# Softmax shift from TensorE to DVE, paired output products and an output bias on POOL, in a fused attention and expert layer

## What is computed

```python
x = x + tanh(g_xattn[0]) * xattn(layernorm(x), ctx)     # 16 heads of 64, causal softmax, scores / sqrt(64)
x = x + tanh(g_ffn[0])   * ffn(layernorm(x))
# ffn, per row, D = 128, 16 "heads" of 8:
h  = rmsnorm(x) * gamma1
q  = h @ Wq + bq;  k, v = split((h @ Wdown + bdown) @ Wup + bup)
att = softmax(q k / sqrt(8)) over the 16 heads of the same row
x2 = x + (att v) @ Wo + bo
h2 = rmsnorm(x2) * gamma2
out = x2 + sum_e softmax(h2 @ Wg + bg)[e] * (h2 @ We[e])   # 8 experts
```

## Time and profile before

| | us |
|---|---|
| median of 3 runs | 261.29 (259.64 to 261.53) |
| the profiled execution | 261.93 |
| its span | 259.9 |

### The profile page before, as it was taken

One profiled execution on the slowest core, in us unless ns is written; L12 is line 12 of the kernel. 1 busy time (PEld: TensorE's weight loads), 2 busy tenths in 40 slices (PEclk: granted clock), 3 DMA queues, 4 the chain that ended last, 5 costly groups with the idle time before them and its releaser, 6 DMA issues.

```text
span 259.9 us, 7887 instructions
## 1 busy us (share of the span) xinstructions
PE 245.6 (94%) x3244; PEld 178.7 (69%) x3244; DVE 192.4 (74%) x333; ACT 171.6 (66%) x501; POOL 149.9 (58%) x157
## 2 busy tenths in 40 slices
PE   7989989998899999999999999988999897979995
PEld 4765877785867677676859595858676462858774
DVE  0237644189998989898998842799989999786964
ACT  2437634756687787978787778566877676472454
POOL 4104041264646686969696835778466995867320
PEclk9999999999999999999999999999999998899999
DMA  6990000000000000000000000000000000000000
GB/s 208 359 320 21 3 4 3 3 1 3 3 3 0 3 10 3 15 0 15 1 3 13 3 11 3 13 3 10 3 0 5 11 14 3 11 0 3 10 13 20
DMA packets 6017, 7.30 MB, mean 28 GB/s; under 512 B 477, under 2 KB 4830, under 8 KB 5982
## 3 DMA queue, kind: packets, MB, share of 16 engines
q1 hardware_dynamic: 5550, 6.16, 7.5%
q10 hardware_dynamic: 432, 0.64, 0.7%
HBM read 5.88 MB, written 0.92 MB: 26 GB/s over the span
## 4 chain that ended last, share of the span: by engine, by line
PE 70%; DVE 18%; ACT 5%; issue 4%; POOL 1%; DVEq 0%; POOLq 0%
PE ps_a L875 40%; PE ps_c L875 9%; PE ps_b L875 8%; PE ps_e L875 7%; PE ps_b L927 4%; DVE ps_e L665 3%; DVE prod L683 3%; DVE ps_e L694 2%; ACT probs L446 2%; DVE nmax L626 2%; PE ps_b L872 1%; DVE psums L631 1%; DVE fqkv L649 1%; POOL prod L326 1%; PE ps_c L971 1%
## 5 line engine op out<-in xcount | busy, mean ns | idle before, releaser
L326 POOL TENSOR_TENSOR prod<-fqkv 128x1280 f32<-128x1280 f32 (+1 forms) x14 | 38.7, 2761 | 10.3 <-DVE fqkv L649 10.3
L316 POOL TENSOR_TENSOR probs<-probs,prinv 120x672 f32<-120x672 f32 x16 | 24.3, 1518 | 31.1 <-DVE prinv L635 31.1
L334 POOL TENSOR_TENSOR prod<-e_sb,fqkv 128x768 f32<-128x768 f32 (+1 forms) x14 | 24.5, 1753 | 21.3 <-ACT e_sb L474 21.3
L875 PEld LDWEIGHTS ps_a<-aT,wo_sb 128*128 128x128 f32 x256 | 30.8, 196 | 4.4 <-ACT v_sb L435 2.6
L875 PE MATMUL ps_a<-aT,wo_sb 128*128 128x112 f32 x256 | 32.1, 279 | 0.4 <-ACT aT L440 0.3
L875 PE MATMUL ps_a<-wv_sb,cT 128*64 128x512 f32 x128 | 32.3, 620 | 0.0
L665 DVE TENSOR_REDUCE ps_e<-prod 128x256 f32<-128x2048 f32 x13 | 29.7, 2287 | 0.0
L694 DVE TENSOR_REDUCE ps_e<-prod 128x128 f32<-128x2048 f32 x13 | 29.7, 2285 | 0.0
L875 PE MATMUL ps_a<-cT,wk_sb 128*128 128x224 f32 x128 | 28.6, 375 | 0.0
L429 ACT COPY kT<-ps_a 128x448 f32<-128x448 f32 x32 | 17.1, 533 | 16.2 <-PE ps_a L875 16.2
L875 PE MATMUL ps_a<-xT,wqc 128*128 128x224 f32 x128 | 27.1, 361 | 0.6 <-ACT qT L429 0.6
(11 more groups left out here) (144 smaller groups left out, 487.9 us busy)
## 6 DMA issues: line engine op xcount, KB each, us to landing
xp_sb<-in_xp SPq DMA_DIRECT2D x1, 896.0 KB, 7.9
out<-out_sb SPq DMA_DIRECT2D x14, 64.0 KB, 1.5
xT<-in_x_t SPq DMA_DIRECT2D x1, 784.0 KB, 9.5
cT<-in_ctx_t SPq DMA_DIRECT2D x1, 784.0 KB, 11.1
wv_sb<-in_wv SPq DMA_DIRECT2D x1, 512.0 KB, 8.1
wo_sb<-in_wo SPq DMA_DIRECT2D x1, 512.0 KB, 12.7
fwe_sb<-in_fwe SPq DMA_DIRECT2D x1, 512.0 KB, 8.8
fw_sb<-in_fw SPq DMA_DIRECT2D x1, 266.0 KB, 13.1
```

Of the source, the lines that this page charges most:

```text
L316: nc.gpsimd.tensor_tensor(pr[0:TG, NC:C, :, 0:S], pr[0:TG, NC:C, :, 0:S], prinv[p % 2][0:TG, NC:C, :].unsqueeze(3).to_broadcast([TG, C - N ...
L326: nc.gpsimd.tensor_tensor(o, k, q, ALU.mult).then_inc(s["prod1_pool"], 1)
L334: nc.gpsimd.tensor_tensor(o, e, v, ALU.mult).then_inc(s["prod2_pool"], 1)
L875: return nc.tensor.matmul(o, lhsT, rhs, start=start, stop=stop, skip_group_check=True)
```

## The change

Five things change, and the order of some calls around them.
1. The shift products go from TensorE. DVE adds the negated maximum, now f32, to the scores in PSUM, in place, right behind the maximum (shifted_scores).
2. The output products (new_y) go by units: pairs (0,1), (2,3), (4,5), (6,7) together, at steps 2, 4, 6 and 8, pairs 8 to 15 alone. aT is one tile of two pairs' width. new_x1 follows the units.
3. A tile starts only when its unit is there: tile 0 at step 2, tiles 1 to 13 at steps 4 to 16, so that step 3 starts none.
4. The bias product goes. ACT multiplies xc by rstd2 (scaled_x), POOL adds the bias to it (biased), and DVE's new_x2 is a plain addition.
5. Orders. POOL makes the output adds before norm, and first_scale last, behind weighted, biased and gating. In steps 14 and 15 scaled_qkv comes before weighted on DVE; in the written-out end some calls swap places.

```diff
@@ units and tiles
-def first_step(f):
-    return (128 * (f + 1) + T - 1) // T
-TILE_AT = {first_step(f): f for f in range(NT)}
-LAST_STEP = first_step(NT - 1) + 2
+DOUBLE = 8
+Y_UNITS = [(p, p + 1) for p in range(0, DOUBLE, 2)] + [(p,) for p in range(DOUBLE, NP)]
+Y_AT = {unit[-1] + 1: n for n, unit in enumerate(Y_UNITS)}
+def units_for(f):
+    return next(n + 1 for n, unit in enumerate(Y_UNITS) if (unit[-1] + 1) * T >= (f + 1) * 128)
+def tile_steps():
+    steps, last = {}, 0
+    for f in range(NT):
+        last = max(last + 1, Y_UNITS[units_for(f) - 1][-1] + 1)
+        steps[last] = f
+    return steps
@@ POOL
+            def biased(f):
+                pool.wait_ge(s["u_ready"], f + 1)
+                if f == 0:
+                    pool.wait_ge(s["wo_scaled"], 2)
+                nc.gpsimd.tensor_tensor(xc[f % XB][:, :], xc[f % XB][:, :], fw_sb[:, COL_BO:COL_BO + D], ALU.add).then_inc(s["ub_ready"], 1)
@@ POOL, steps 2 to 13
                 if fb is not None:
                     products(fb)
+                if fd is not None:
+                    outputs(fd)
                 if t < NP:
                     norm(t)
                 if fc is not None:
                     second_scale(fc)
                 if fb is not None:
                     weighted(fb)
+                    biased(fb)
+                if fc is not None:
+                    gating(fc)
                 if fa is not None:
                     first_scale(fa)
-                if fc is not None:
-                    gating(fc)
-                if fd is not None:
-                    outputs(fd)
@@ ACT
+            def scaled_x(f):
+                act.wait_ge(s["centred"], f + 1)
+                act.wait_ge(s["rstd2_ready"], f + 1)
+                nc.scalar.activation(xc[f % XB][:, :], xc[f % XB][:, :], ACT.Copy, scale=rstd2[f % XB][:, 0:1]).then_inc(s["u_ready"], 1)
@@ ACT, steps 2 to 13
                     head_exps(fb)
+                    scaled_x(fb)
                 if t < NP:
                     turned_probs(t)
+                if fc is not None:
+                    gate_exps(fc)
                 if fa is not None:
                     x1_copy(fa)
-                if fc is not None:
-                    gate_exps(fc)
                 if t < NP:
                     attended(t, 0)
+                if fc is not None:
+                    experts(fc, 0)
+                    experts(fc, 1)
+                if t < NP:
                     attended(t, 1)
@@ DVE
+            def shifted_scores(p):
+                sc = score_banks(p)[0:TG, :, 0:C * S].rearrange("p r (c k) -> p r c k", c=C)
+                dve.wait_ge(s["nmax_ready"], p + 1)
+                nc.vector.tensor_tensor(sc, sc, nmax[p % 2][0:TG, :, :].unsqueeze(3).to_broadcast([TG, 2, C, S]),
+                                        ALU.add).then_inc(s["shifted"], 1)
@@ DVE, new_x2
-                nc.vector.scalar_tensor_tensor(out=x2[f % 2][:, 0:D], in0=xc[f % XB][:, :], scalar=rstd2[f % XB][:, 0:1], in1=ps_c[:, 1, 0:D],
-                                               op0=ALU.mult, op1=ALU.add).then_inc(s["x2_ready"], 1)
+                dve.wait_ge(s["ub_ready"], f + 1)
+                nc.vector.tensor_tensor(x2[f % 2][:, 0:D], ps_c[:, 1, 0:D], xc[f % XB][:, :], ALU.add).then_inc(s["x2_ready"], 1)
@@ DVE, steps 14 and 15
                 score_max(t)
+                shifted_scores(t)
                 products(fb)
+                prob_sums(t)
                 new_x2(fc)
-                prob_sums(t)
+                new_x1(Y_AT[t])
                 norm(t)
                 logits(fb)
-                new_x1(t - 1)
                 gate_logits(fc)
                 shifted_logits(fb)
+                scaled_qkv(fa)
                 weighted(fb)
...
@@ DVE, the end
                 scaled_qkv(last)
+            shifted_logits(prior)
             products(last)
-            shifted_logits(prior)
@@ TensorE
-            def shift(p):
...
+            def new_y(n):
+                if n == 0:
+                    pe.wait_ge(s["wo_in"], 16)
                 for b in range(2):
+                    pe.wait_ge(a_free[b], USES["y", n][b])
+                if n:
+                    pe.wait_ge(s["x1T_ready"], n)
+                c0, w = Y_UNITS[n][0] % 2 * T, len(Y_UNITS[n]) * T
                 for ch in range(C):
+                    ins = mm(ps_a[:, 0, 0:w], wo_sb[:, ch, :], aT[:, ch, c0:c0 + w], start=(ch == 0), stop=(ch == C - 1))
                 ins.then_inc(s["y_made"], 1)
...
@@ TensorE, steps 2 to 13
                     scores(t)
                     values(t, 0)
-                    values(t, 1)
                 if fc is not None:
                     turn_o(fc)
                 if t < NP:
-                    shift(t)
-                if fc is not None:
-                    bias_o(fc)
+                    values(t, 1)
+                if fc is not None:
                     new_o(fc)
-                if t <= NP:
-                    new_y(t - 1)
+                if t in Y_AT:
+                    new_y(Y_AT[t])
@@ TensorE, the end
             logit_sums(prior)
+            output_sums(PE_OUT[0])
             turn_x2(third)
-            output_sums(PE_OUT[0])
+            expert_half(third, 1)
             gate_logits(third)
-            expert_half(third, 1)
```

More of the change, by code:

```diff
@@ L408, in _ @@
             gating(third)
+            biased(prior)
             weighted(last)
             second_scale(prior)
+            biased(last)
             gating(prior)
@@ L439, in attended @@
                 act.wait_ge(a_full[b], n)
[L440 removed]
+                nc.scalar.copy(aT[:, 4 * half:4 * half + 4, p % 2 * T:(p % 2 + 1) * T],
                                ps_a[:, b, 0:4 * T].rearrange("p (c t) -> p c t", c=4)).then_inc(a_free[b], 1)
@@ L541, in _ @@
                 if t < NP:
+                    values(t, 0)
                     exps(t)
@@ L587, in _ @@
             kv_copy(last)
-            x2_copy(third)
             squares(third)
             head_exps(prior)
-            late_out(PE_OUT[0])
+            scaled_x(prior)
+            x2_copy(third)
+            scaled_x(last)
             gate_exps(third)
             head_exps(last)
+            late_out(PE_OUT[0])
             experts(third, 1)
@@ L603, in _ @@
             x2_copy(last)
+            experts(prior, 1)
             experts(prior, 0)
-            experts(prior, 1)
             gate_exps(last)
@@ L850, in _ @@
             shifted_logits(last)
+            gate_sum(third)
             head_scales(prior)
-            gate_sum(third)
             normed_heads(prior)
             weighted(last)
+            head_scales(last)
             new_x2(prior)
-            head_scales(last)
             head_sums(last)
@@ L859, in _ @@
             gate_logits(prior)
+            new_x2(last)
             gate_sum(prior)
-            new_x2(last)
             gate_logits(last)
@@ L1159, in _ @@
             turn_o(prior)
-            bias_o(prior)
             new_o(prior)
```

118 lines of the change are left out of this document (49 added, 69 removed).

## The result

The changed kernel takes 264.08 us (median of 4 runs, 263.70 to 264.89); the kernel before, timed beside it, 260.47 (259.52 to 261.53). The ratio is 1.016, 95% interval 1.012 to 1.020. The prediction was 259.2 with a range up to 263.3, so the kernel is slower, by less than 2%, where I forecast about the same or faster, and it lies outside the range. The profiled execution of after was timed at 263.70; its span is 261.9 against 259.9 before. One later run of before (263.40) and one of the kernel with the first pair alone (265.38) were in a slower state of the chip and are left out of all figures.

What follows compares the result with a forecast made beforehand. Full steps were taken as TensorE-bound before, thin steps and the end as DVE-bound; afterwards DVE's work sets full steps. Step terms sum to -3.6 us, 261.29 to 257.7, plus 1.5 for one clock fall: 259.2 us, range 256.2 to 263.3.

Steps and rivals of the forecast that it cites:

- Pairs 9 to 13, five steps of 13.7: Full single-unit steps late in the kernel: 13.7 us each on 13.6 of DVE work, +0.2 us in all against 68.3.
- Wrong if full steps exceed 14.2: Stated sign of failure: a full step, from one pair's maximum to the next, longer than 14.2 us.
- loop through POOL: Query scaling, POOL's products, output adds and norm, then TensorE to the next scores: 27.4 us over two steps, 13.7 each.
- My upper bound, 14.9: Single-unit full step if the shift comes wholly on top: 13.95 + 1.04 - 0.06 us.
- TensorE's saving of 0.61 a step: Full step with a single unit: shift 0.38 and bias product 0.23 us leave TensorE, 13.95 to 13.34.
- Pair 2, +0.6: Pair 2's step, 12.0 us before: double unit for a single one and no shift, +0.6 us.
- The fall of the clock, +1.5: Thin steps 3 and 5: TensorE's clock falls to half at 1 to 2 us per fall; one counted, +1.5.
- The shift's price: DVE's new instruction on 896 elements in PSUM: 1.1 us, expected to show at 1.08 to 1.17.
- DVE over 97% busy: Expected sign: in full steps of 13.6 to 13.8 us DVE is over 97% busy and TensorE idles again.
- Before pair 2, -2.4: Prologue: unit 0 leaves, 2.02 us, with attend(1)'s 0.6 wait; two DVE shifts add 0.15; less 2.4 us.
- The end, -1.4: Pair 15 -0.6 us and the rest -0.8, from query scaling ahead of the head sums and fewer bias products.
- Rival 3: Full steps of 14.6 us, late POOL output adds and DVE not absorbing the shift: 264.9 us; chance 0.13.

Runs made afterwards that it cites:

- the first pair alone: The kernel before, with the output projections of pairs 0 and 1 as one unit in step 2; 262.30 us, ratio 1.009.
- x1 ahead: The changed kernel, with DVE making x1 ahead of the norm in steps 2 to 13, as before; 262.75 us, ratio 1.009.
- eleven heads: The changed kernel with x1 made ahead of the norm, POOL multiplying 11 instead of 10 heads in tiles 0 to 9; 265.41 us, ratio 1.019.
- the shift alone: The kernel before, with only the shift moved to DVE behind the maximum (f32 maximum); 266.10 us, ratio 1.021.
- the bias alone: The kernel before, with only the output bias changed: no bias product, ACT scales, POOL adds the bias, DVE adds the product; 264.03 us, ratio 1.013.
- eight narrow products: The changed kernel, with eight unused narrow products added ahead of pair 2's step, 32 TensorE records more; 263.54 us, ratio 1.012.
- the narrow warm-up: The changed kernel, with 28 products of 32 columns for the two wide ones of TensorE's warm-up; 275.09 us, ratio 1.055.
- both kernels of the first pair: The kernel before with pairs 0 and 1 as one unit, without (262.30 us) and with eight unused narrow products where the prologue's output products stood (259.26 us).

## Why the prediction was wrong, step by step

- **Pairs 9 to 13, five steps of 13.7: the step that failed.** They take 14.10 to 14.24 without gaps, and 14.37 on average in after. "Wrong if full steps exceed 14.2" was my own sign, and it came. Three things in it were wrong. (1) I had DVE's 13.6 of work as the length of the step. The work is 13.5 to 13.7, but DVE's own row takes 13.84 (x1 ahead): hand-overs of 0.02 to 0.1 us between instructions that need each other come on top. (2) I looked at a loop through POOL and not at the one through x1: x1 stands behind the norm, the shift and the norm are ahead of it, and the projections wait for the bank that it reads. That is 0.37 us a step (shown by the run with x1 ahead). (3) The norm beside POOL's output adds costs DVE 0.15 in after, up to 0.5 (shown by the run with eleven heads). The loop through x1 is thus 5.50 us on DVE and 8.61 on TensorE, 14.11, with the norm alone, and 14.24 with the norm at 0.53. The loop through POOL that I priced at 13.7 is not on the chain of pair 10's or 11's step; it is on that of pair 7's, which has no unit and takes 13.69 where I had 12.9 to 13.3. My upper bound, 14.9, held this, but I took the value near the lower bound, on the strength of idle time that the shift would fill. It did fill it (the run with the shift alone).
- **TensorE's saving of 0.61 a step.** The chain gives 13.64 for its row of work with x1 ahead, against 13.95: 0.31. The shift's 0.38 is real. The bias was priced 0.23 as half of 0.46 for two products; with the bias gone the output product alone takes 0.42. In before's order that is the wait for ACT's copy of oT, in whose shadow the bias product stood (the run with the bias alone). In after's order oT is there 0.6 us before the product starts (166.07 and 166.70 with x1 ahead), and why it takes 0.42 all the same is not shown. And the value products, split by turn_o, take 0.15 more. Only DVE being the bound kept this error out of the time.
- **Pair 2, +0.6.** Without its gap (the run of after with eight narrow products) the step takes 13.00 where I had 12.6, and 12.69 with the narrow warm-up; the gap is the other 1.3 to 1.7. I had no term for it, and the trace of before gave little sign of one: its only trace of it is 0.3 us in the scores ahead of pair 6. Other kernels lose more by such gaps: the first pair alone 4.45 us in three.
- **The fall of the clock, +1.5.** None in the profiled execution of after, whose pair 3 was at 1.00 with TensorE busy 9.24 of 13.17. It came in that step, at 0.88 to 0.90, in the seven other kernels here that have step 3 without a tile, and cost 1.0 to 1.2 there (in five of them the step took 14.1 to 14.2 instead of 13.17, in two the loss fell on pair 4's). The three other runs of after, at 263.9 to 264.9, had a mean clock of 0.993 where the profiled one had 1.00. So the forecast place is right for most runs, and the size, 1.5, was somewhat high. That the profiled run had none is luck. By the rule of the Trainium skill that I cited (TensorE: Matmul & The Clock Gate, "What's actually happening") step 5 would have fallen too; in no run here did it, with TensorE busy 10.0 to 10.6 of 13.6 to 13.8.
- **The shift's price.** Right: 1.10 us, within 1.08 to 1.17, no wait before new_x2, as forecast. "DVE over 97% busy" was 95% (68.2 of 71.9).
- **Before pair 2, -2.4.** -3.4; the kernels with the first pair alone have -2.0 to -3.8, with the same work. The first maximum lies at 15.4 to 16.7 us in kernels that have the same work ahead of it (15.70 in after, 16.64 in before), so up to 1.3 is how soon the first projections end behind the loads. From that maximum to pair 2's the unit is worth 1.9 to 2.6, 2.5 in after: the term is right, and 0.9 of the 3.4 is luck.
- **The end, -1.4, measured -1.7.** Right in size by luck, wrong in cause. Before's rest holds the fall of the earlier trace rows. In both kernels of the first pair, which have before's orders there but no such fall, it takes 42.3 to 42.4 of the same work instead of 43.6. After's 41.9 is 0.4 better than that, and its step 14 is 0.4 longer. The reordered end brought nothing.
- **Rival 3** named the outcome, slower full steps from 14.15 on, at 264.9. Its mechanism, late output adds, is not what was seen: in the steps of pairs 9 to 13 TensorE never waits for POOL (once behind the prologue, 0.2 us, in pair 7's).

Of the 2.0 us by which the span grew, then: before pair 2 -3.4, pair 2 +2.3 (1.3 to 1.7 its gap, the rest its double unit), pairs 3 to 8 +0.9, pairs 9 to 13 +3.6, the end with pair 14 -1.3, nearly all of it before's fall of the clock. The 3.6 can be told apart roughly, by my estimate from the rows: scores that come late 0.8 (0.31 and 0.49 in the steps of pairs 10 and 12), x1 behind the norm 5 x 0.37 = 1.8, and DVE's row of 13.84 in place of before's mean of 13.67 with its thin place of step 9 (13.23) 0.9. No run has both x1 ahead and full steps without gaps or a fall, so that these three add up is argued and not shown.

## What to carry to other kernels

When work goes from a full engine to one with idle time, the idle time does not tell whether the step gets shorter: write down the loops that go through both engines, from one maximum to the next, with every buffer that the second engine must release. Here the shift fitted into DVE and lay in series with TensorE all the same. And before a gap of a microsecond or two without a releaser is put down to the change, count the instructions up to it in several variants: a handful of unused ones ahead of it can tell whether it is the work or where the instruction stream is cut. Profile more than one execution, since the same instructions had gaps in one and not in the other.

## What the hardware showed that I had not expected

- TensorE stood still for 0.2 to 1.97 us in or just behind dense runs of 64x56 products, at records 192 or 193 beyond a multiple of 256, with a packet of the instruction queue 2.2 to 2.9 us before the end of each large gap. Of some 25 ends of pieces in a kernel none to five give a gap. Why some packets come late (in after 5 us behind the end before, in before 1 us there), and whether the packet is what TensorE waits for, is open.
- DVE's norm, a product of two operands in SBUF, slows beside POOL's additions in SBUF: 0.39 us alone, 0.54 in after, 0.89 wholly beside one that starts 0.08 us before it and takes 0.73. Waiting for the end of POOL's instruction and then working would give 1.04 and, in pair 10's step of after, 0.68; the rows have 0.15 less each time. The Trainium skill (SBUF — State Buffer, "Who interferes with whom") says that a DVE instruction with two SBUF inputs contends with a GpSimd instruction that reads SBUF, and that the contention is an exclusive lock. The rows agree (0.39 alone, up to 0.89 beside POOL's additions), and I should have priced POOL's moved additions by it.
- Fp32 products of 32 columns with 128 x 128 weights took 217 ns each in a row (56 in 12.15 us) at the start of the kernel, while the 64x56 ones, nearly as narrow, take 16 later on (64 in 1.00 us). The two places are not alike: the two wide products that stand at the start in after took 3.28 us for 1,792 columns, where an expert half later takes 0.86 for 1,024. But products of 112 columns with such weights take 0.11 each there (16 in 1.77), seven times a 64x56 one's share.
